# A decoder layer on one core: activation tables requested ahead of their use, expert weights issued ahead of their second biases, and the last batch's expert rows written to token rows

## The reference, cut

```python
x = x + attn(_layernorm(x), Wk, Wq, Wv)               # one causal head of 128
x = x + xattn(_layernorm(x), ctx, ctx, mask, ...)     # 16 heads of 8, 154 context tokens
x = x + ffn(_layernorm(x), ...)
# ffn, inside:
q, k, v = heads(x @ Wq + bq), heads(x @ Wk + bk), heads(x @ Wv + bv)   # 16 heads of 8
q = q * cos + _rotate_half(q) * sin                                    # k too
ao = softmax(q k^T / sqrt(8)) v
x1 = _layernorm(x + ao @ Wo + bo) * g1 + be1
gate_probs = softmax(x1 @ Wg + bg); topk_p, topk_i = top_k(gate_probs, 2)
comb = one_hot(topk_i) weighted with topk_p / sum(topk_p)
h = gelu(x1 @ W1[e] + b1[e]); y = h @ W2[e] + b2[e]                    # 8 experts, 512 hidden
return _layernorm(x1 + sum_e comb[e] * y[e]) * g2 + be2
```

## Time and profile before

| | |
|---|---|
| median of 3 runs | 685.74 us (682.94 to 687.5) |
| the profiled execution, its own time | 684.35 us |
| its span | 682.6 us |
| busy: PE, DVE, ACT, POOL | 608.9 us (89%), 453.7 (66%), 345.6 (51%), 121.5 (18%) |
| chain that ended last | PE 61%, DVE 20%, ACT 6%, issue 5%, POOL 3%, SP 2% |
| mean granted clock of PE | 0.975 |

### The profile page before, as it was taken

How to read it: one execution, slowest core, us unless ns; L and a number is a source line. 1 busy time by engine, 2 the same in 40 slices (tenths; PEclk the granted TensorE clock), 3 DMA queues, 4 the chain that set the end, 5 groups by cost and what they waited for, 6 DMA issues and landing times.

```text
span 682.6 us, 11214 instructions
## 1 busy us (share of the span) xinstructions
PE 608.9 (89%) x4086; PEld 386.0 (57%) x4086; DVE 453.7 (66%) x1126; ACT 345.6 (51%) x618; POOL 121.5 (18%) x121
## 2 busy tenths in 40 slices
PE   6899899999998999999998989999999999886960
PEld 3664454437645764468836754478647644376950
DVE  4673588937854779657836778677726689479224
ACT  0405126874144458866254568755435488552530
POOL 5100100001041200001053400031136100220433
PEclk8999999999999999999999999999999999988985
DMA  6300000001025460003146640012155610126861
GB/s 205 124 0 1 1 0 2 1 1 39 1 92 162 138 181 2 1 1 110 29 123 174 186 121 1 1 39 64 36 171 153 203 54 2 31 79 192 281 177 42
DMA packets 45085, 54.98 MB, mean 81 GB/s; under 512 B 4346, under 2 KB 35432, under 8 KB 45032
## 3 DMA queue, kind: packets, MB, share of 16 engines
q1 hardware_dynamic: 43240, 50.61, 25.4%
q0 software_dynamic: 1792, 3.67, 1.8%
HBM read 46.73 MB, written 7.54 MB: 80 GB/s over the span
## 4 chain that ended last, share of the span: by engine, by line
PE 61%; DVE 20%; ACT 6%; issue 5%; POOL 3%; SPq 2%; DMA 1%; POOLq 0%; DVEq 0%; ACTq 0%
PE banks L1810 8%; PE banks L1796 5%; PE banks L1455 5%; PE banks L1441 5%; PE banks L1777 4%; DVE nm L1263 3%; PE banks L1759 3%; PE banks L1660 3%; PE banks L1692 2%; PE banks L1690 2%; ACT px L900 2%; PE banks L1663 2%; POOL rstd L615 2%; DVE hat L947 2%; PE banks L1709 2%
## 5 line engine op out<-in xcount | busy, mean ns | idle before, releaser
L1263 DVE TENSOR_REDUCE nm<-banks 128x1 fp32r<-128x512 f32 x256 | 157.7, 681 | 23.9 <-PE banks L1777 23.4
L900 ACT ACTIVATE px<-banks 128x1024 f32<-128x1024 f32 x128 | 127.8, 1026 | 21.3 <-PE banks L1796 21.3
L723 ACT ACTIVATE hT<-banks,wp 128x128 f32<-128x128 f32 x216 | 61.6, 370 | 60.8 <-PE banks L1441 60.5
L615 POOL TENSOR_TENSOR rstd<-ve,misc 128x4 f32<-128x4 f32 x19 | 19.5, 1028 | 404.8 <-DVE ve L941 404.8
L1777 PE MATMUL banks<-kst,qst 32*128 32x512 f32 x256 | 81.8, 495 | 1.5 <-ACT kst L873 0.8
L1810 PE MATMUL banks<-px,vf 128*32 128x256 f32 (+1 forms) x832 | 76.7, 440 | 5.6 <-ACT ot L906 2.5
L1441 PE MATMUL banks<-xT,wp 128*128 128x128 f32 x432 | 59.8, 282 | 4.1 <-ACT hT L723 2.7
L1796 PE MATMUL banks<-q2st,kst 32*128 32x512 f32 x256 | 59.1, 495 | 2.8 <-ACT px L900 2.8
L1455 PE MATMUL banks<-wp,hT 128*128 128x128 f32 x432 | 59.3, 282 | 2.1 <-ACT hT L723 2.1
L1441 PEld LDWEIGHTS banks<-xT,wp 128*128 128x128 f32 x432 | 53.9, 194 | 10.8 <-issue 5.2
L1455 PEld LDWEIGHTS banks<-wp,hT 128*128 128x128 f32 x432 | 54.4, 197 | 3.5 <-ACT hT L723 2.7
(11 more groups left out here) (283 smaller groups left out, 1030.5 us busy)
## 6 DMA issues: line engine op xcount, KB each, us to landing
wp<-in_experts SPq DMA_DIRECT2D x54, 514.0 KB, 4.6
b2r<-in_L_ffn_b SPq DMA_DIRECT2D x53, 64.0 KB, 4.3
px<-in_experts SPq DMA_DIRECT2D x6, 514.0 KB, 6.1
expert_rows<-xs SPq DMA_DIRECT2D x12, 256.0 KB, 5.1
xs<-expert_tokens SPq DMA_DIRECT2D x9, 256.0 KB, 3.0
msk<-in_mask SPq DMA_DIRECT2D x4, 308.0 KB, 3.2
xin<-in_x SPq DMA_DIRECT2D x4, 256.0 KB, 2.9
ot<-in_const_sel SPq DMA_DIRECT2D x1, 1024.0 KB, 5.1
```

The source lines that it names most:

```text
L615: pool.tensor_tensor(rstd[:, n, :], ve[:, n, :], exponent, ALU.pow).then_inc(k[f"ln_rstd{n}"], 1)
L723: ins = act.activation(hT[:, n % 2, c * P:(c + 1) * P], bank[h_bank(p, i)][:, c * P:(c + 1) * P], ACT.Gelu, bias=weights(n, 2 * FF + c, 2 ...
L900: act.activation(px[:, c % 2, 2 * i:2 * i + 2, :], banks[:, 4 + 2 * i:6 + 2 * i, :], ACT.Exp, scale=SCALE_H).then_inc(k["f_exp"], 1)
L1263: dve.tensor_reduce(nm[:, t, g, BLK * hh:BLK * hh + 1], bank[s1_bank(g, t, i)], AX.X, ALU.max, negate=True).then_inc(k["f_max"], 1)
```

## The change

Six things are changed.

1. `load_table(func)` on ACT: an activation of one column of `euler` into a scratch column, so that the table load of `func` stands at that place. It is called with Exp in the opening (once `zeroed` is complete), ahead of the first q2st copy of cross attentions 1 to 3 and of self attentions 1 to 3, and with Gelu behind the exps of cross attentions 1 to 3 and in the last tail. Eleven calls; the table load ahead of "ta" stays.
2. Batch 3's weights: SP issues the weights of its first eight tiles without their biases, with the two `keep_y` of batch 2 among them; then the eight biases, each with a `value_load` of its own; then a load of row numbers.
3. Batch 3's results: eight indirect DMAs on POOL (`send_ids`) write for each slot the row of the token it belongs to; SP loads that table (`row_of`). As each group is added, POOL writes its tiles to `token_rows` in DRAM at these rows (`send_rows`, 15 indirect DMAs, straight from `ysb`; unused slots go to rows of their own behind). In place of four `keep_y` and eight fetches, SP loads four pieces of `token_rows` in token order. POOL's order becomes: numbers, batch 2's fetches, rows of groups 0 and 1, batch 2's power (`rstd_of(4, 2)`), rows of groups 2 and 3, batch 3's power.
4. DVE: three small operations make the numbers (`noted`), behind the second placing. The last group of batch 3 is added tile by tile, into alternating banks. The end of batches 2 and 3 is `end_rows`: (mixed - mean) * g2 ahead of the wait for the power, then times rstd plus x2b, four tiles each, and the output leaves in two halves for batch 3.
5. PE: in the opening, keys, queries and values stand ahead of the wait for the small loads and the bias columns; in cross attentions 1 to 3 `down(p, 0)` stands ahead of the turning of hat3; batch 0's gate logits stand ahead of the query stacks. DVE's copy of the bias columns moves behind the values accordingly.
6. SP loads one more constant, and fills `slot_rows` in DRAM from a constant; waits on `xs_zeroed` count both.

```diff
@@ sync: load_expert
                 sp.dma_start(weights(n, 0, WP),
                              experts_in[bass.DynSlice(e, 1)].rearrange("e p c -> (e p) c")).then_inc(w_in[w_slot(n)], 16)
+                if n < NT * (B - 1) or i >= WSLOTS + WMORE:
+                    load_bias(p, i, e)
+
+            def load_bias(p, i, e):
                 g = NG * p + i // YG
                 if g >= 2 and b2_place(g) < 2:
                     sp.wait_ge(k["y_out"], g - 1)
...
@@ sync: the loop over batches
                     for i in range(YG):
                         load_expert(B - 1, i)
                     keep_y(p, NG - 2)
+                    for i in range(YG, WSLOTS + 1):
+                        load_expert(B - 1, i)
                     keep_y(p, NG - 1)
-                    for i in range(YG, WSLOTS + WMORE):
+                    for i in range(WSLOTS + 1, WSLOTS + WMORE):
                         load_expert(B - 1, i)
-                else:
+                    for i in range(WSLOTS + WMORE):
+                        load_bias(B - 1, i, sp.value_load(eid[0:1, (B - 1) % 2, i:i + 1], min_val=0, max_val=NE - 1))
+                    sp.wait_ge(k["xs_sent"], 16 * 2 * T * B)
+                    sp.dma_start(row_of[:], row_dram.rearrange("(s i) o -> s (i o)", s=P)).then_inc(k["slots_loaded"], 16)
+                elif p < B - 1:
                     for g in range((NT - ahead) // YG, NG):
                         keep_y(p, g)
-            sp.wait_ge(k["out_ready"], B)
-            sp.dma_start(out[B - 1].rearrange("(t p) d -> p t d", p=P), outb).then_inc(k["out_stored"], 16)
-            sp.wait_ge(k["out_stored"], 16 * B)
+            sp.wait_ge(k["out_stored"], 16 * (B - 1))
+            for i in range(2):
+                sp.wait_ge(y_sent[i], 16 * sum(min(YG, NT - YG * g) for g in range(i, NG, 2)))
+            for t in range(T):
+                sp.dma_start(yg[:, :, t, :], yt_dram[0:2 * S].rearrange("(j t p) d -> p j t d", j=2, p=P)[:, :, t, :],
+                             ).then_inc(xs_in[t], 16)
+            for i in range(2):
+                sp.wait_ge(k["out_ready"], B - 1 + 2 * (i + 1))
+                sp.dma_start(out[B - 1].rearrange("(t p) d -> p t d", p=P)[:, 2 * i:2 * i + 2, :],
+                             outb[:, 2 * i:2 * i + 2, :]).then_inc(k["out_stored"], 16)
...
@@ gpsimd
+            def send_rows(i):
+
+                g = i // YG
+                n = NG * (B - 1) + g
+                if i == 0:
+                    pool.wait_ge(k["slots_loaded"], 32)
+                if i % YG == 0 or g == NG - 1:
+                    pool.wait_ge(k["y_out"], n + 1 + i % YG * (g == NG - 1))
+                pool.indirect_dma_start(yt_dram, bass.IndirectOffsetOnAxis(row_of[:, i:i + 1], 0),
+                                        ysb[:, n % 2, i % YG, :], None).then_inc(y_sent[g % 2], 16)
...
@@ scalar
+            def load_table(func):
+
+                i = next(table_columns)
+                act.activation(table_out[:, i:i + 1], euler[:, 0:1], func)
...
@@ vector: end
+            def end_rows(p):
+
+                dve.wait_ge(k["x2b_ready"], p + 1)
+                own.wait()
+                for t in range(T):
+                    own.inc(dve.scalar_tensor_tensor(yg[:, 0, t, :], yg[:, 0, t, :], mean[:, 4, t:t + 1], vecs[:, VEC_G2, :],
+                                                     ALU.subtract, ALU.mult))
+                dve.wait_ge(k["ln_rstd4"], p + 1)
+                own.wait()
+                for t in range(T):
+                    ins = dve.scalar_tensor_tensor(outb[:, t, :], yg[:, 0, t, :], rstd[:, 4, t:t + 1], x2b[:, p % 2, t, :],
+                                                   ALU.mult, ALU.add)
+                    if p == B - 1 or t == T - 1:
+                        ins.then_inc(k["out_ready"], 1)
...
@@ tensor: down, and cross
+                at = y_bank(p, g)
+                if p == B - 1 and g == NG - 1:
+                    at = last_y_bank(i % YG)
+                    if i % YG:
+                        pe.wait_ge(k["y_out"], NG * p + g + i % YG - 1)
...
-                turn_rows(2, n, hat3, 0)
                 if p >= 0:
                     down(p, 0)
+                turn_rows(2, n, hat3, 0)
```

More of the change, by code:

```diff
@@ L251, in q2_bank, with build @@
     return RING_ORDER.index((g,)) % RING
-def build(nc, x, ctx_in, mask, w, consts, experts_in, xs_dram, ys_dram, out):
+def build(nc, x, ctx_in, mask, w, consts, experts_in, xs_dram, ys_dram, row_dram, yt_dram, out):
     stack = ExitStack()
@@ L414, in build @@
         y_back = [sem(f"y_back{t}") for t in range(T)]
+        y_sent = [sem(f"y_sent{i}") for i in range(2)]
         block = stack.enter_context(nc.Block())
@@ L570, in _ @@
                     done = i - ahead + 1
-                    if done % YG == 0:
+                    if done % YG == 0 and p < B - 1:
                         keep_y(p, done // YG - 1)
@@ L704, in _ @@
             affine_rows(B - 1)
-            pool.wait_ge(k["g_slots"], B)
+            send_ids()
             fetch_tokens(B - 2)
-            finish(B - 2)
-            fetch_tokens(B - 1)
+            for i in range(2 * YG):
+                send_rows(i)
+            rstd_of(4, B - 2)
+            for i in range(2 * YG, NT):
+                send_rows(i)
             rstd_of(4, B - 1)
@@ L794, in tail @@
                     gelus(p - 1, "tb")
+                if not ahead:
+                    load_table(ACT.Gelu)
                 if after:
@@ L827, in opening @@
                 act.wait_ge(k["zeroed"], 11)
+                load_table(ACT.Exp)
                 context_copies(0, 7, 6)
@@ L841, in cross @@
                     gelus(p - 1, label)
+                if n:
+                    load_table(ACT.Exp)
                 act.wait_ge(k["x_q2_mm"], G * n + 1)
@@ L853, in cross @@
                     act.activation(pxt[:, g % 2, :], bank[2], ACT.Exp, scale=SCALE_H).then_inc(k["x_expt"], 1)
+                if p >= 0:
+                    load_table(ACT.Gelu)
                 gelus(p, "w0")
@@ L891, in self_attention @@
                 gelus(b - 1, "o3")
+                if b:
+                    load_table(ACT.Exp)
                 copy_q2(0)
@@ L956, in add_biases @@
                     dve.wait_ge(b2_in[b2_place(n)], 16 * b2_loads(n))
-                    if n >= 2:
+                    if p == B - 1 and g >= 2:
+                        dve.wait_ge(y_sent[n % 2], 16 * YG)
+                    elif n >= 2:
                         dve.wait_ge(y_kept[n % 2], 16 * (n // 2))
@@ L961, in add_biases, with add_last_biases @@
                                       biases(n, 0, width), ALU.add).then_inc(k["y_out"], 1)
+            def add_last_biases():
+                n = NG * B - 1
+                dve.wait_ge(b2_in[b2_place(n)], 16 * b2_loads(n))
+                dve.wait_ge(y_sent[n % 2], 16 * YG)
+                for j in range(NT - YG * (NG - 1)):
+                    dve.wait_ge(k["y_part"], NT * (B - 1) + YG * (NG - 1) + j + 1)
+                    dve.tensor_tensor(ysb[:, n % 2, j, :], bank[last_y_bank(j)][:, j * D:(j + 1) * D],
+                                      biases(n, j, j + 1)[:, 0, :], ALU.add).then_inc(k["y_out"], 1)
             def normalise_heads(t, b, i, heads_bank):
@@ L1380, in _ @@
             place_tokens(1)
+            dve.wait_ge(k["g_slots"], B)
+            own.inc(dve.tensor_scalar(slot_parts[:, 0, :], slot[:, (B - 1) % 2, :], P - 1, None, ALU.bitwise_and))
+            own.inc(dve.tensor_scalar(slot_parts[:, 1, :], slot[:, (B - 1) % 2, :], 7, None, ALU.logical_shift_right))
+            own.wait()
+            dve.scalar_tensor_tensor(noted[:], slot_parts[:, 0, :], float(NT), slot_parts[:, 1, :], ALU.mult,
+                                     ALU.add).then_inc(k["g_noted"], 1)
             for g in range(1, NG):
@@ L1644, in tail @@
                     experts(p - 1, "tf")
+                if p == 0:
+                    gate_logits(p)
                 if ahead:
                     x_query_stacks(n)
-                if after:
+                if p > 0:
                     gate_logits(p)
@@ L1978 @@
     rows = [nc.dram_tensor(f"expert_rows{i}", (NT * P, D), F32, kind="Internal").ap() for i in range(2)]
+    slot_rows = nc.dram_tensor("slot_rows", (NT * P, 1), _mybir.dt.int32, kind="Internal").ap()
+    token_rows = nc.dram_tensor("token_rows", (2 * S + NT * P, D), F32, kind="Internal").ap()
     out = nc.dram_tensor("out_0", (B, S, D), F32, kind="ExternalOutput").ap()
-    build(nc, x, ctx, mask, w, consts, experts, tokens, rows, out)
+    build(nc, x, ctx, mask, w, consts, experts, tokens, rows, slot_rows, token_rows, out)
     r = _run(nc, [arrays], core_ids=[0])
```

62 lines of the change are left out of this document (40 added, 22 removed).

## The result

The changed kernel takes 681.83 us in the median of nine runs, the kernel before 684.97: a ratio of 0.9944 (0.9925 to 0.9963), 3.1 us between the medians where 9 were predicted. On another chip it was 0.9934 (0.991 to 0.9957).

The account below looks back on a forecast made before the run. PE was taken to bound the four batches, then the last batch's weights and tail. Gains of 3.7 and 5.3 us sum to 9.0, giving 675.3 us profiled and 676.7 us median, range 672.5 to 681 (8 in 10).

Parts of the forecast that it names:

- The tail: Last batch, from group 2's addition to the end: 22.9 us instead of 28.16, a gain of 5.3 us.
- T: Moment when DVE has added group 2 of the last batch; forecast at 654.4 us, no gain and no loss.
- Output 2.78: Last step of the tail: the output after DVE's last steps takes 2.78 us, as in the kernel before.
- The weights: Last batch's weights ahead of biases: PE's 4.65 us stall at tile 1 only moves to tile 8; no gain.
- The order on PE: PE's new order: opening 1.3 us, down of tile 0 0.8 us, gate logits minus 0.3 us.
- The opening: Keys and queries start 1.6 us earlier, bias columns cost back 0.3: gain 1.3 us (0.5 to 1.6).
- Down of tile 0: Ahead of turning hat3 it fills an idle stretch, avoiding batch 1's half clock: gain 0.8 us (0 to 1.7).
- The gate logits: Batch 0's, moved ahead of the query stacks, partly delay these: minus 0.3 us (0 to minus 0.96).
- The tables: Early ACT table loads: each of three in self attention costs 0.65 us, so 1.9 us gained.
- Rival (c): Gains in the batches do not carry; opening and attentions end at another engine's wait: 679.2 us, 10 of 100.
- rival a: Port lock: DVE's placings and POOL's eight sends hold each other up by 4.7 us: 679.3 us, 22 of 100.
- Rival (b): The weights are no bound; POOL sets group 2's addition at 652.2 us: 673.6 us total, 15 of 100.

Follow-up runs that it names:

- first profile: The changed kernel, profiled after the change; span 683.2 us, against 682.6 us for the kernel before.
- second profile: The changed kernel profiled on another chip: span 680.9 us, ratio to the kernel before 0.9934.
- the weights were mended: Changed kernel with tiles 8 and 9's weights ahead of biases 0 to 5, last root on ACT, batch 0's gate logits back behind query stacks: 0.9869 to the kernel before.
- the repairs: Changed kernel with last root on ACT, tiles 8 and 9's weights ahead of biases 0 to 5, batch 0's gate logits behind query stacks: 677.85 against 686.49 us before.
- an experiment of its own: Changed kernel with 16 more indirect DMAs on POOL: 0.9955; with the last root on ACT instead of POOL: 0.9892; changed kernel beside them 0.9934, all to the kernel before.

## Why the prediction was wrong

**The tail, 5.3 predicted.** T to the end measured 24.7, not 22.9; before 28.16. The steps up to the output were right: last send over at T+8.9 (8.65), loads issued at T+10.3 (9.9), power at T+17.5 (17.2), last rows at T+19.8 (20.1). The step that failed is "Output 2.78": it took what DVE's last operation and the end had between them before for a cost of the output, though POOL's drain of 5.75 us stood hidden in the same place, and did not ask what fifteen more indirect DMAs do to it. That was 1.8 us of the tail, and 2.1 of the whole by the end's distance. The Trainium skill (VectorE: DVE Perf Modes, "The DRAIN you can't avoid") tells of the flush behind each DVE operation and of drains of about 12 ns on all engines that come from the preamble and postamble. The ones here stand at a line of the program and are neither: the row took 7 ns on SP, and 5.75 to 8.33 us on POOL.

**The weights, 0 predicted on T.** The mechanism was right in its main parts: no stall at tile 1, one at tile 8, eight biases of 1.1 us, and on an undisturbed chip no gain. Mis-sized was the stall. Tile 8's weights left at 638.79 and 637.97, where 636.9 was forecast. And the prediction took 4.1 us from issue to PE's start, from tile 1, whose weights had only biases beside them; behind eight biases and the row numbers it was 5.96 in the first profile and 5.25 in the second. Then it took 1 us for the half clock, where three pieces cost about 2.5 in the first profile and two pieces 1.8 in the second. T moved by +1.0 us in the second profile and +3.4 in the first, against the kernel's own last cast of eid. That the transfers ahead in the queue make the landing long was argued, not tested. What the prediction did not have is that the down of tile 7, and so group 1, waits with tile 8, and that the row numbers reach POOL 5 to 6 us behind their issue: POOL's power stood at 654.3 and 652.7 where 649.8 was forecast. So both of its bounds on T moved out together.

**The order on PE, 1.8 predicted.** The opening gives 0.7 to 1.4, as said (alone 1.9 in the time, 0.6 to 3.1; the first profile shows a loss of 0.9, since it has the late fall), but a granted clock that falls at one of several places decides more than the edit. The failed step is "Down of tile 0 ... **0.8 us**": it took one execution's fall in batch 1 for a property of the idle stretch. The gate logits cost 0.44 for 0.3.

**The tables, 1.9 predicted.** 1.5 in the stretches, nothing measurable in the time. Rival (c) had that at 10 of 100, too little.

**POOL and the port (rival a).** The eight sends beside DVE's placings took 0.96 to 1.30 us in the first profile and 1.02 to 1.70 in the second, against 0.947, and one placing 1.90 for 1.67: 1.2 and 1.9 us on POOL's queue. T didn't hang on it, since POOL stood waiting for the row numbers behind its fetches. The Trainium skill's rule on DVE blocking POOL's descriptors (SBUF — State Buffer, the box on "DVE blocks DMA") fits these rows, but no run here tests that it is their cause, and it cost no more than that. That POOL bounds T from below at about 652 was right in kind, and was seen once the weights were mended (group 2 at 653.2, held by the power). Rival (b), without a bound by the weights, was forecast at 673.6, 12.1 us off the kernel before, and was not reached even by the repairs with the drain gone too: 8.6 us off.

So of 9.0 us: 1.8 went to the drain, 1 to 3 to tile 8, 0.9 to down of tile 0 and the gate logits, up to 1.9 to tables whose time did not carry, and in the first profile 2 more to a fall of the clock that its partner did not have in that place. Of these the drain is shown by an experiment of its own; the shares of the others are read from single profiles.

## What to carry to other kernels

Read the closing instructions of every engine before you cost a tail: a drain that is hidden today is the bound once what hides it gets shorter, and on POOL it grew with each indirect DMA of the whole program. When a load is moved ahead of others, ask which later load now leaves behind them, and take its landing from one that had as much in front of it. A stall or a half clock seen in one profile is not the kernel's until a second profile shows it.

## What the runs showed that I had not expected

POOL's closing drain: 5.75, 7.02 and 8.33 us for 56, 71 and 87 indirect DMAs, 5.753 to 5.755 in all ten profiles with 56, and 7.022 to 7.025 in all six with 71 and the power behind them. The fall of the clock in the opening came near 10 us, near 32 us or not at all with one and the same order of the opening, and moved the rest of the execution by up to 2.3 us. On two of the chips all kernels took 17 to 21 us more with three stops, one of which ended for ACT and DVE within 0.03 us, and there an edit worth nothing elsewhere was worth 2 to 5 us.
